# A two-layer graph network on one core: layer 0 projected side by side, layer 1's coefficients in three column groups

## What is computed

```
layer 0:  msg = sum over 9 coefficients c of edge:  s_c * (h[src] @ W_c)          W_c: 32 x 32
          x  += segment_sum(msg, dst)
layer 1:  a   = tanh(relu((h[src] @ A1' + b1) . (h[dst] @ A2' + b2 + rel[type]) / sqrt(32)))
          msg = a * sum over 16 bases b of wcomp[type, b] * (h[src] @ V_b)
          x  += relu(segment_sum(msg, dst) + h[src of the last edge] @ W_self)
```

## Time and profile before

| | us |
|---|---|
| median of 3 runs | 4632.38 (4622.65 to 4634.9) |
| the profiled execution | 4637.38 |
| its span, first to last instruction | 4635.5 |
| mean granted clock of PE | 0.851 |

### The profile page before, as it was taken

One profiled execution on the slowest core, in us unless ns is written; L12 is line 12 of the kernel. 1 busy time (PEld: TensorE's weight loads), 2 busy tenths in 40 slices (PEclk: granted clock), 3 DMA queues, 4 the chain that ended last, 5 costly groups with the idle time before them and its releaser, 6 DMA issues.

```text
span 4635.5 us, 106735 instructions
## 1 busy us (share of the span) xinstructions
PE 3578.4 (77%) x41254; PEld 3052.1 (66%) x41254; DVE 2689.9 (58%) x3863; ACT 1097.0 (24%) x2563; POOL 2301.7 (50%) x2427
## 2 busy tenths in 40 slices
PE   3788888888888888885677777777777777777777
PEld 2677777777777777775566666666666666666666
DVE  5455555555555555555555665656656665556565
ACT  1111111111111111112233333333333333333332
POOL 5555555555555555553344444544444444445442
PEclk9889988888988989997788888888888888888887
DMA  3111111111111111111122222222222222222221
GB/s 102 21 21 20 20 21 19 20 20 21 20 20 21 20 20 21 21 20 54 35 38 39 38 37 38 40 37 37 37 41 37 38 39 38 37 37 39 39 37 35
DMA packets 216608, 150.09 MB, mean 32 GB/s; under 512 B 121048, under 2 KB 197261, under 8 KB 216079
## 3 DMA queue, kind: packets, MB, share of 16 engines
q0 software_dynamic: 77504, 39.84, 8.9%
q1 hardware_dynamic: 137999, 100.77, 8.8%
q10 hardware_dynamic: 576, 2.40, 0.1%
HBM read 134.58 MB, written 8.22 MB: 31 GB/s over the span
## 4 chain that ended last, share of the span: by engine, by line
PE 38%; issue 13%; another core or an unknown queue 2%; DVE 1%; ACT 1%; ACTq 0%; DVEq 0%
PE ps L636 20%; PE ps L717 7%; PE ps L649 5%; PE ps L675 2%; PE ps L699 1%; PE ps L687 1%; PE ps L599 0%; ACT p_left L846 0%; PE ps L619 0%; DVE room L1095 0%; DVE row_var L969 0%; ACT p_left L886 0%; DVE squares L996 0%; DVE H L966 0%
## 5 line engine op out<-in xcount | busy, mean ns | idle before, releaser
L564 POOL DMA_INDIRECT xg<-h_table,idx x2422 | 2290.8, 946 | 2272.7 <-PE ps L717 1530.1
L636 PE MATMUL ps<-h,blocks 128*128 128x448 f32 x9856 | 2284.3, 388 | 43.3 <-DVE blocks L1024 29.2
L636 PEld LDWEIGHTS ps<-h,blocks 128*128 128x128 f32 x9856 | 1937.9, 202 | 262.8 <-issue 76.6
L1024 DVE TENSOR_TENSOR blocks<-scratch,ps 128x896 fp32r<-128x896 int16 x704 | 761.2, 1082 | 882.8 <-remote 864.7
L717 PE MATMUL ps<-room,xg 128*32 128x42 f32 (+2 forms) x21882 | 699.4, 267 | 301.5 <-issue 297.4
L717 PEld LDWEIGHTS ps<-room,xg 128*32 128x32 f32 x21882 | 579.6, 144 | 429.0 <-issue 412.4
L1033 DVE SCALAR_TENSOR_TENSOR scratch<-ramp_sb,scratch,ps 128x448 f32<-128x448 f32 x704 | 476.4, 677 | 512.1 <-remote 250.7
L649 PE MATMUL ps<-att_tab,p_left 128*128 128x49 bf16 x4689 | 261.2, 200 | 555.3 <-issue 553.7
L1095 DVE TENSOR_TENSOR room<-coef,ps 128x756 f32<-128x756 f32 (+1 forms) x522 | 648.9, 1284 | 4.9 <-DVE ps L1044 0.2
L649 PEld LDWEIGHTS ps<-att_tab,p_left 128*128 128x128 bf16 x4689 | 201.6, 107 | 610.5 <-issue 609.5
L880 ACT ACTIVATE p_left<-ps 96x504 f32<-96x504 f32 (+2 forms) x262 | 168.8, 644 | 1200.8 <-PE ps L717 1200.7
(11 more groups left out here) (108 smaller groups left out, 1144.5 us busy)
## 6 DMA issues: line engine op xcount, KB each, us to landing
xg<-h_table,idx POOLq DMA_INDIRECT x2422
rows_b<-typ_short SPq DMA_DIRECT2D x130, 258.0 KB
scratch<-q_short SPq DMA_DIRECT2D x260, 96.0 KB
rows_b<-dst_short SPq DMA_DIRECT2D x130, 126.0 KB
coef<-in_edge_dram SPq DMA_DIRECT2D x130, 54.0 KB
att_tab<-p_table SPq DMA_DIRECT2D x393, 8.1 KB
p_table<-room SPq DMA_DIRECT2D x8, 297.0 KB
X<-in_x_dram SPq DMA_DIRECT2D x7, 224.0 KB, 4.3
```

The costliest lines, as they stand in the source:

```text
L564: pool.indirect_dma_start(xg[:, g.q, t - g.s * J, :], None, h_table[n], bass.IndirectOffsetOnAxis(ap=idx[:, t:t + 1], axis=0)).then_inc(L. ...
L636: last = pe.matmul(found_ps[b], blocks[:, b, c, :], h_2[:, a, c], start=(c == 0 and a == 0), stop=(c == NCH - 1 and a == 1))
L1024: dve.tensor_tensor(blocks[:, b], q_b[:, g.b, i, :].unsqueeze(1).broadcast_to([P, NCH, P]), block_ps.unsqueeze(2).broadcast_to([P, NCH, P] ...
```

## The change

Layer 0 takes layer 1's way of projecting. Three matmuls with stationary weights (96 x 32) and 168 moving columns go side by side in three column groups; ACT copies `oT`; `sum_quarters` adds the three groups; ACT copies `o`, now 32 columns wide. The centred copy is made by DVE from `o` (`centre`, a reduction and a product), at the end of its step behind `spread`, and `place_rows` waits for that. In layer 0 `sum_quarters` stands behind the second found tile, ahead of the third. The weights' centred half is no longer prepared.

Layer 1 splits its 17 coefficients over three column groups, 6, 6 and 5: a tile takes matmuls of 84, 84 and 70 columns. The projection has six chunks, five of 96 rows and one of 64, in four column groups. PE finds 340 tiles there, which were 322.

```diff
-NP = [[2 if s < 8 else 3 for s in range(FULL)], [2 if s < 8 else 3 if s == FULL - 1 else 3 - s % 2 for s in range(FULL)]]
+NP = [[2 if s < 8 else 3 for s in range(FULL)], [2 if s < 8 or s == FULL - 2 else [2, 3, 3][s % 3] for s in range(FULL)]]
...
-QS = [[0, 3, 6, 9, 9], [0, 5, 9, 13, 17]]
-CQ = [3, 5]
-NQ = [3, 4]
+QS = [[0, 3, 6, 9, 9], [0, 6, 12, 17, 17]]
+CQ = [3, 6]
+NQ = 3
+CHUNK = [[3 * F, 3 * F, 3 * F], [3 * F, 3 * F, 3 * F, 3 * F, 3 * F, 2 * F]]
...
-                def project(g):
...
                 def project_in_quarters(g):
...
                     for c in range(cq):
-                        rows, q = (P, c) if c < MQ else (F, 0)
+                        rows, q = CHUNK[n][c], c % MQ
                         last = pe.matmul(oT_ps[q * F:(q + 1) * F, 0:hh * w], weights[0:rows, c, :], G_sb[0:rows, c, 0:hh, 0:w],
-                                         start=(c < MQ), stop=(c > 0), tile_position=(0, q * F))
+                                         start=(c < MQ), stop=(c + MQ >= cq), tile_position=(0, q * F))
...
                 def sum_quarters(g):
...
+                    rows = min(cq, MQ) * F
                     for h in range(hh):
-                        last = pe.matmul(o_ps[0:w, h, 0:no], oT_sb[:, h, 0:w], four_units[:], start=True, stop=True)
+                        last = pe.matmul(o_ps[0:w, h, :], oT_sb[0:rows, h, 0:w], four_units[0:rows, :], start=True, stop=True)
...
                 def place_rows(g):
...
-                    pe.wait_ge(L.o_set, g.order())
+                    pe.wait_ge(L.centred if n == 0 else L.o_set, g.order())
...
                 def sum_edges(g, back):
...
-                        for q in range(NQ[n]):
+                        for q in range(NQ):
...
                 def step(gs):
                     tiles = gs[0].found_tiles(n) if gs[0] else []
                     find_rows(tiles[0:1])
+                    if gs[2]:
+                        project_in_quarters(gs[2])
+                    find_rows(tiles[1:2])
                     if n == 0 and gs[2]:
-                        project(gs[2])
-                    if n == 1 and gs[2]:
-                        project_in_quarters(gs[2])
-                    find_rows(tiles[1:])
+                        sum_quarters(gs[2])
+                    find_rows(tiles[2:])
                     if n == 1 and gs[2]:
                         sum_quarters(gs[2])
...
                 def copy_G(g):
...
-                    if n == 1:
-                        act.activation(to[0:F, :, cq - 1, :], bank[0:F, :, cq - 1, 0:w], ACT.Copy)
-                    chunks, rows = min(cq, MQ), NQ[n] * F
-                    act.activation(to[0:rows, :, 0:chunks, :], bank[0:rows, :, 0:chunks, 0:w], ACT.Copy).then_inc(L.G_set, 1)
+                    whole = CHUNK[n].count(NQ * F)
+                    if whole < cq:
+                        rows = CHUNK[n][whole]
+                        act.activation(to[0:rows, :, whole, :], bank[0:rows, :, whole, 0:w], ACT.Copy)
+                    rows = NQ * F
+                    act.activation(to[0:rows, :, 0:whole, :], bank[0:rows, :, 0:whole, 0:w], ACT.Copy).then_inc(L.G_set, 1)
...
                 def step(gs):
...
-                    if n == 1 and gs[2]:
+                    if gs[2]:
                         copy_oT(gs[2])
...
+                def centre(g):
+                    hh, w = g.halves()
+                    dve.wait_ge(L.o_set, g.order())
+                    wait(dve, L.centred, g.order() - 1)
+                    dve.tensor_reduce(o_sum[0:w, 0:hh], o_sb[0:w, 0:hh, 0:F], AX_X, ALU.add).then_inc(L.o_sum_set, 1)
+                    dve.wait_ge(L.o_sum_set, g.order())
+                    wait(dve, L.placed, g.order() - 1)
+                    dve.scalar_tensor_tensor(out=o_sb[0:w, 0:hh, F:2 * F], scalar=-1.0 / F, op0=ALU.mult, op1=ALU.add,
+                                             in0=o_sum[0:w, 0:hh].unsqueeze(2).broadcast_to([w, hh, F]),
+                                             in1=o_sb[0:w, 0:hh, 0:F]).then_inc(L.centred, 1)
...
                     if old:
                         spread(old)
+                    if n == 0 and gs[2]:
+                        centre(gs[2])
...
-            dve.tensor_tensor(w0c[:, :, 0:F], w0_sb[:], cg_sb[:], ALU.mult).then_inc(w0_set, 1)
-            dve.wait_ge(w0_set, 1)
-            dve.tensor_reduce(w0_sum[:], w0c[:, :, 0:F], AX_X, ALU.add).then_inc(w0_set, 1)
-            dve.wait_ge(w0_set, 2)
-            dve.scalar_tensor_tensor(out=w0c[:, :, F:2 * F], in0=w0_sum[:].unsqueeze(2).broadcast_to([P, CQ[0], F]),
-                                     scalar=-1.0 / F, in1=w0c[:, :, 0:F], op0=ALU.mult, op1=ALU.add).then_inc(w0_set, 1)
+            dve.tensor_tensor(w0c[:], w0_sb[:], cg_sb[:], ALU.mult).then_inc(w0_set, 1)
```

More of the change, by code:

```diff
@@ L217, in build @@
         oT_ps = ps[:, 4, 0:2 * HW]
-        o_ps = ps[0:HW, 4, 2 * HW:2 * HW + 4 * F].rearrange("p (h o) -> p h o", h=2)
-        win_ps = ps[0:3 * F, 4, 2 * HW + 4 * F:2 * HW + 4 * F + P]
+        o_ps = ps[0:HW, 4, 2 * HW:2 * HW + 2 * F].rearrange("p (h o) -> p h o", h=2)
+        win_ps = ps[0:3 * F, 4, 2 * HW + 2 * F:2 * HW + 2 * F + P]
         found_ps = [ps[:, 5 + b, 0:MC * F].rearrange("p (f m) -> p f m", f=F) for b in range(2)]
@@ L239, in build @@
         w0_sb = sb("w0_sb", [P, CQ[0], F])
-        w0c = sb("w0c", [P, CQ[0], 2 * F])
-        w0_sum = sb("w0_sum", [P, CQ[0]])
+        w0c = sb("w0c", [P, CQ[0], F])
         w1_sb = sb("w1_sb", [P, CQ[1], F])
@@ L284, in build @@
         is_node, first_node, node_step = (node_cols[:, i:i + 1] for i in range(3))
+        o_sum = sb("o_sum", [HW, 2])
         coef0 = sb("coef0", [P, 2, J, C0])
@@ L385, in __init__ @@
                     self.coef_in = [sem(f"coef_in{n}_{b}") for b in range(2)]
+                    self.o_sum_set = sem(f"o_sum_set{n}")
+                    self.centred = sem(f"centred{n}")
                 if n == 1:
@@ L650, in attention_rows @@
                     last.then_inc(L.ex_done, 1)
-                def project(g):
-                    hh, w = g.halves()
-                    pe.wait_ge(L.G_set, g.order())
-                    wait(pe, L.o_set, g.order() - 1)
-                    wait(pe, L.added, g.order() - 1)
-                    for h in range(hh):
-                        for c in range(cq):
-                            rows = NQ[n] * F
-                            last = pe.matmul(o_ps[0:w, h, 0:no], G_sb[0:rows, c, h, 0:w], weights[0:rows, c, :],
-                                             start=(c == 0), stop=(c == cq - 1))
-                    last.then_inc(L.turned, 1)
                 def project_in_quarters(g):
@@ L761, in _ @@
             last.then_inc(q_turned, 1)
-            pe.wait_ge(w0_set, 3)
+            pe.wait_ge(w0_set, 1)
             pe.wait_ge(pw_set, 1 + MQ)
@@ L827, in edge_copies @@
                 cq = CQ[n]
-                no = OUT[n].stop - OUT[n].start
                 def attention(g):
@@ L885, in copy_oT @@
                     wait(act, L.turned, g.order() - 1)
-                    act.activation(oT_sb[:, 0:hh, 0:w], oT_ps[:, 0:hh * w].rearrange("p (h w) -> p h w", h=hh),
+                    rows = min(cq, MQ) * F
+                    act.activation(oT_sb[0:rows, 0:hh, 0:w], oT_ps[0:rows, 0:hh * w].rearrange("p (h w) -> p h w", h=hh),
                                    ACT.Copy).then_inc(L.oT_set, 1)
@@ L892, in copy_o @@
                     wait(act, L.placed, g.order() - 1)
-                    act.activation(o_sb[0:w, 0:hh, 0:no], o_ps[0:w, 0:hh, 0:no], ACT.Copy).then_inc(L.o_set, 1)
+                    act.activation(o_sb[0:w, 0:hh, 0:F], o_ps[0:w, 0:hh, :], ACT.Copy).then_inc(L.o_set, 1)
                 def step(gs):
```

## The result

| | before | after |
|---|---|---|
| median, us | 4632.35 (4 runs) | 4795.92 (4793.75 to 4802.99, 4 runs) |
| ratio | | 1.036, 95% interval 1.0341 to 1.0378 |
| span of the profiled execution | 4635.5 | 4801.1 |
| mean granted clock of PE | 0.851 | 0.836 |

The change costs 163.6 us. The forecast was 4707, with 4765 as the upper end: the direction was right, the size was not.

The account below looks back on a forecast made before the run. PE was taken as held up by POOL's gather bursts, coming free about 2 us after each, not bound by its own work. Terms -24 + 60 + 39 = +75 on 4632 gave 4707 us, 1.6% slower; range 4600 to 4765.

Parts of the forecast that it names:

- The law of the step: Both layers: a step is 0.87 us, 1.25 a gather, about 2, then PE's work still left behind the crawl.
- The crawl: PE's hole with only single records starting, in layer 1's attention rows and layer 0's sums; ends about 2 us after the gathers.
- Groups: +60: Layer 1's sums: three wider column groups cost 0.46 us in each of 131 steps, behind the crawl.
- Tiles: -24: Layer 1: 18 more found tiles turn 18 ten-gather steps into nine-gather ones, 19.21 to 17.86 us each; extra PE work covered.
- Layer 0's chain: +39: Layer 0's project, copy, sum, copy, centre, place: 0.3 us a step over 131 steps, from bounds 0 to 0.7.
- the 607.2 us: ACT's L893 wait before 125 layer 0 copies, over half "remote"; read as slow messages to ACT while gathers run.
- the chain wholly exposed: Layer 0 rival, 14%: ACT's copy of o not served before PE's crawl, each step pays 0.7 us; 4760 in all.
- width paid: Layer 1's sums: the widest column group sets the price, so wider groups cost; with layer 0's chain hidden 4668, 22%.

Follow-up runs that it names:

- layer-0-alone run: Changed kernel with layer 1 put back as before; ratio to the kernel before 1.0183 with the crawl (4639.07 us), 1.0062 without.
- groups-alone run: Kernel before with only layer 1's three column groups and six chunks; ratio 1.0149 with the crawl (4623.81 us), 1.0016 without.
- tiles-alone run: Kernel before with only layer 1's 340 found tiles for 322; ratio 1.0009 with the crawl (4556.64 us), 1.0114 without.
- run 38: Not a run number: the words are "tiles-alone run" followed by a count, 38 steps of three tiles with nine gathers, 17.70 us each.
- The late placing: Changed kernel with layer 0's rows placed behind the last tile of the sums, not the fourth; 4530.37 us, 0.994 of the kernel before.
- the run with four gathers: Kernel before with four gathers a group for nine or ten, other rows not loaded; 3191.57 us for 4555.12, ratio 0.7012.

## Why the prediction was wrong

**The law of the step: right.** Step = 0.87, 1.25 us a gather, about 2 us, and what is behind. The crawl goes with the burst (0.7012), and its end stays 1.6 to 2.2 us behind the last gather in the mean, in before, after and the parts. Work ahead of the crawl is free as far as its time goes: layer 0's projection got shorter, and no step did by it.

**Groups: +60, measured +68 (60 to 76).** The stage at half clock was 3.80 us in the changed kernel by the mean of 54 such stages, for 3.24 before; a difference of 0.56 was forecast. The mean stage went up by 0.42 between before and after, for 0.46 taken. But where the groups alone differ in layer 1 (the layer-0-alone and the groups-alone run, same chip) it went from 2.94 to 3.21, up by 0.27 only, since many stages had a higher clock than half there (0.71 in the mean of the three-tile steps). Not in the sum were the attention rows left behind the crawl, +0.24 to +0.33 us a step. So the size came out near by luck: the width cost less than was taken on that chip, and a term that was put at nothing made up for it. I had said of the projection's sixth chunk that it is covered. But PE gets as far as a certain place in its instructions, the 120th to 130th of the step (matmuls and weight loads) in the steps looked at of the groups-alone and the layer-0-alone run; four more ahead are four fewer done when the crawl ends. By the 1.49 us of 32 records above that is 0.1 us; the rest isn't accounted for.

**Tiles: -24, measured +4 (-2 to +10).** The swap "18 steps with ten gathers become steps with nine" took step and burst as one pair. The burst that runs beside a step is of the group two on. With two and three in turn, a three-tile step always had a nine-gather burst. With two, three, three it is so in one case of three: in the tiles-alone run 38 steps of three tiles with nine gathers take 17.70 us, 38 of two with nine 17.70, and 39 of three with ten 19.36, the dearest, where before the ten-gather steps of two tiles took 18.98 and the nine-gather ones 17.38 (the layer-0-alone run, same chip). The gain of fewer bursts of ten went into that: the mean of the steps is 18.25 for 18.18.

**Layer 0's chain: +39, measured +83 (76 to 91).** This is the step that failed. "I take 0.3 of 0 to 0.7, nearer to the low end because PE's sum is done some 3 us ahead of the crawl": the sum is done, 3.4 us ahead of the last gather in the step shown, but the room is of no use, since ACT isn't served in it. In the mean its copy came 1.9 us after the last gather, and in 2 of 127 steps ahead of it. The trace of before had shown this in layer 1, and not in layer 0. ACT's copy of `o` in the step of the earlier trace rows:

```profile
1023.80 0.27 ACT L893 ACTIVATE p_left<-ps 84x128 f32<-84x128 f32 x1 [4.70 <-remote]
```

In layer 0 before, the copy began 1.7 us behind the projection and 5.2 us ahead of the last gather, in every step looked at (113): the 607.2 us of the earlier trace rows are ACT with nothing to do, and no sign of a late copy, as the prediction read them. In layer 1, where PE's sum ended 9.3 us into the step, the copy came 5.4 us behind it and 2.3 us behind the last gather, in none of 113 steps ahead of it. The new sum of layer 0 ends 8.2 us into the step and met the same: 5.3 us to the copy. I gave that case, the chain wholly exposed, 14%. Its price of 0.7 us was about right in size (0.56 to 0.77), but not its make-up: it isn't the wait alone, but also what stands behind it, the half clock in the sums among it, and it is paid because the placing stands ahead of the sums that release the gathers' buffer. The late placing shows it: it leaves the late copy as it is and takes nearly all of the cost away.

Wholly exposed, width paid and -24 for the tiles was 4760; with the tiles at +4 and the groups at +68 it is 4796. That this meets the measured time to the microsecond is luck, since it has layer 0 at +92: the parts as measured are 83, 68 and 4, together 155 of the 164.

## What to carry to other kernels

When one engine has holes that end at another's clock, first ask where the release of the buffer stands which starts that other engine's work, and put nothing ahead of its last reader that can stand behind: in the changed kernel, moving one placing of 1 us there gave more than the whole change took (0.994 for 1.0375 of the time before). A new link in a chain gets no credit for time in which its engine isn't served; see what a message of the same kind did in the same stretch of a step. And pair each step with the transfers that run beside it, not with those of its own group.

## What the chip showed that I had not expected

The same kernel took 3153 us on two chips of this type and 4555 to 4642 on the others, each within 0.6% of its own median, and with equal durations of the single gather (946 ns in the mean on both). Where it takes longer, PE nearly comes to a stand while POOL issues gathers one behind the other, its records (matmuls and weight loads) then 0.7 us or twice that apart, and what PE tells ACT late in the burst is acted on only behind it. What it tells early in the burst isn't held up so: the copies at 1133.87 and 1023.80 in the rows above. From the timeline of the changed kernel in layer 1:

```profile
3022.50 0.18 PE L652 MATMUL ps<-att_tab,p_left 128*128 128x49 bf16 x1 [2.14 <-issue]
3023.92 0.10 PEld L652 LDWEIGHTS ps<-att_tab,p_left 128*128 128x128 bf16 x1 [2.76 <-issue]
3024.62 0.20 PE L652 MATMUL ps<-att_tab,p_left 128*128 128x49 bf16 x1 [1.94 <-issue]
```

By the view of cores, the kernel before with the crawl and the groups-alone run without it:

```profile
core 0: 4635.5 us, clock 0.851
```
```profile
core 0: 3156.2 us, clock 0.987
```

The packets of 16 KB of the instruction queue q8 do not take longer where there is a crawl: 335 in the profile of before, 1.10 us each in the mean, and 313 of 1.11 us in the groups-alone run. The Trainium skill (Runtime: NRT & Kernel Launch, Instruction fetch mechanics) has the crossing of such a block mostly hidden. The durations are alike in the two runs, crawl or none; whether a packet comes too late, and so whether the trace agrees, no row here shows.

The traces with the crawl also hold fewer events of semaphores: 21,587 in before for 62,222 in the groups-alone run, and 27,536 in the run with four gathers, which has no crawl but is of such a chip. So some of what stands there as "issue" or "remote" may be a wait whose sender was lost, and a releaser named so is weak evidence. What the cause of the crawl is, no run here settles. Bursts of four gathers do not bring it on, bursts of seven do, and with it goes the clock: less crawl, more full clock behind it in these runs.
